# Normalised rows of the first five images on ScalarE, a third input place, and a new order

## The reference

```python
xn = rmsnorm(ln_c(x), g_norm)                  # ln_c: over channels
q, k, v = W_qkv @ xn                           # 4 heads of 32
q = softmax over the head's 32 dims; k = softmax over the 1024 tokens
out = W_out @ (context(k, v) applied to q) + b_out
x = x + rmsnorm(out, g_out)
t = tokens of x
xf = (t - mean) / sqrt(var + 1e-5)             # ln_t: over the 128 channels of a token
probs = softmax(xf @ gate_w + gate_b); the two best of 8 experts per token
t = t + sum over the two of prob * (gelu(xf @ w1[e] + b1[e]) @ w2[e] + b2[e])
```

## Time and profile before

| what | value |
|---|---|
| median of three runs | 755.87 us (751.54 to 756.84) |
| profiled execution | 758.1 us, span 756.4 us |
| PE busy | 658.9 us, 87% |
| DVE busy | 562.6 us, 74% |
| ACT busy | 535.5 us, 71% |
| POOL busy | 481.0 us, 64% |
| mean granted TensorE clock | 0.94 of full |
| HBM traffic | 103.81 MB read, 57.02 MB written |

### The profile page before, as it was taken

How to read it: one execution, slowest core, us unless ns; L and a number is a source line. 1 busy time by engine, 2 the same in 40 slices (tenths; PEclk the granted TensorE clock), 3 DMA queues, 4 the chain that set the end, 5 groups by cost and what they waited for, 6 DMA issues and landing times. The chain is left out here.

```text
span 756.4 us, 15759 instructions
## 1 busy us (share of the span) xinstructions
PE 658.9 (87%) x4074; PEld 545.3 (72%) x4074; DVE 562.6 (74%) x2178; ACT 535.5 (71%) x1388; POOL 481.0 (64%) x504
## 2 busy tenths in 40 slices
PE   3867689889899798999879989998899899998995
PEld 2553478768588577977758867876789788887884
DVE  5889879999899987999778889788679522332342
ACT  2643348787787597879869778686698765676764
POOL 1002635717777677777767777777777775777773
PEclk9987779999999899999989999999699999999997
DMA  7801358458777776896667978884799899659622
GB/s 176 227 19 39 129 183 251 139 175 262 228 201 233 226 230 189 250 271 208 224 218 228 277 224 233 238 262 147 218 282 308 280 294 345 203 149 288 205 78 84
DMA packets 110208, 159.28 MB, mean 211 GB/s; under 512 B 19216, under 2 KB 74536, under 8 KB 110120
## 3 DMA queue, kind: packets, MB, share of 16 engines
q1 hardware_dynamic: 93704, 126.58, 54.7%
q0 software_dynamic: 15360, 31.49, 13.9%
q10 hardware_dynamic: 1056, 0.22, 0.2%
HBM read 103.81 MB, written 57.02 MB: 213 GB/s over the span
## 5 line engine op out<-in xcount | busy, mean ns | idle before, releaser
L840 POOL DMA_INDIRECT rows_in<-xf_tok,row_of x240 | 242.8, 1012 | 179.3 <-DVE row_of L1401 90.9
L855 POOL DMA_INDIRECT y_rows<-rows_out,row_back x240 | 235.8, 982 | 84.6 <-issue 76.5
L1640 PE MATMUL y_ps<-wb,hid 128*128 128x128 f32 x1552 | 207.2, 283 | 17.2 <-ACT hid L957 15.9
L1640 PEld LDWEIGHTS y_ps<-wb,hid 128*128 128x128 f32 x1552 | 189.5, 194 | 36.4 <-ACT hid L957 33.3
L957 ACT ACTIVATE hid<-h_ps,wb 128x256 f32<-128x256 f32 x388 | 162.2, 474 | 55.7 <-PE h_ps L1630 53.1
L1630 PE MATMUL h_ps<-xt,wb 128*128 128x256 f32 x648 | 171.3, 389 | 7.0 <-DMA wb<-experts 5.8
L1630 PEld LDWEIGHTS h_ps<-xt,wb 128*128 128x128 f32 x648 | 114.8, 196 | 21.2 <-DMA wb<-experts 6.9
L1468 DVE TENSOR_TENSOR yb<-y_ps,wb 128x256 f32<-128x256 f32 x162 | 68.0, 420 | 81.2 <-PE y_ps L1640 80.0
L1550 PE MATMUL ab<-wqkv_t,x_sb 128*128 128x392 f32 x256 | 107.8, 556 | 11.9 <-ACT xt L951 4.8
L943 ACT ACTIVATE y_rows<-y_rows,share 128x128 f32<-128x128 f32 x240 | 80.9, 406 | 34.1 <-DMA y_rows<-rows_out,row_back 33.7
L895 ACT ACTIVATE qkv<-ab,root 128x392 f32<-128x392 f32 x128 | 72.4, 589 | 32.7 <-PE ab L1550 26.1
(11 more groups left out here) (195 smaller groups left out, 970.0 us busy)
## 6 DMA issues: line engine op xcount, KB each, us to landing
wb<-experts SPq DMA_DIRECT2D x162, 321.0 KB
xb<-rows_in SPq DMA_DIRECT2D x162, 128.0 KB
rows_out<-yb SPq DMA_DIRECT2D x162, 128.0 KB
rows_in<-zeros SPq DMA_DIRECT2D x69, 128.0 KB, 2.8
x_sb<-in_x_dram SPq DMA_DIRECT2D x16, 512.0 KB, 4.4
out_dram<-out_sb SPq DMA_DIRECT2D x32, 256.0 KB, 3.0
rows_in<-xf_tok,row_of POOLq DMA_INDIRECT x240
y_rows<-rows_out,row_back POOLq DMA_INDIRECT x240
```

The lines of the kernel that those rows point to most:

```text
L840: pool.indirect_dma_start(out=rows_in[p % IN_BUFS], out_offset=bass.IndirectOffsetOnAxis(ap=row_of[:, n % X1_RING, k, t:t + 1], axis=0), i ...
L855: pool.indirect_dma_start(out=y_rows[:, r, k, :], out_offset=None, in_=rows_out[p % OUT_BUFS][0:BLOCKS[p] * ROWS, :], in_offset=bass.Indir ...
L1640: last = pe.matmul(y_ps[:, b % Y_BUFS, i * P:(i + 1) * P], hid[:, b % 2, k, i * P:(i + 1) * P], wb[:, r, HIDDEN + k * CH:HIDDEN + (k + 1) ...
```

## The change

For images 0 to 4 (AIDED = 5) the rows xf are written by ACT as root * x1 + shift, with `shift2` = -mean * root from one new small instruction on DVE. From image 5 on DVE writes them as before; it waits once, at image 5, until ACT has written those of image 4, so that `s_xf` counts in order. POOL's sends wait for the first half of xf before their first tile and for the second before their fifth. `x_sb` has three places in place of two, each with its semaphore. `cw_t` no longer has memory of its own but lies in `square`. All bonuses have new values, so every engine's list may have a new order. The planner gets a few more dependences between steps of neighbouring images.

```diff
-X_RING, TOK_RING, QKV_RING, PAIR_RING = 2, 3, 2, 3
+X_RING, TOK_RING, QKV_RING, PAIR_RING = 3, 3, 2, 3
+AIDED = 5
 ...
-FAVOURED = {...}, FAVOURED_KIND = {...}
+other values for nearly all
 ...
+        if n < AIDED:
+            step("DVE", a("shift2"), 0.1, [a("pair_r")] + old("xf1", 2), 0.12)
         for h in range(2):
-            before = [a("xf0")] if h else [a("pair_r")] + chain("xf1")
+            before = [a("xf0")] if h else [a("shift2" if n < AIDED else "pair_r")] + chain("xf1")
 ...
-            step("DVE", a(f"xf{h}"), 1.02, before, 0.1)
+            step("ACT" if n < AIDED else "DVE", a(f"xf{h}"), 1.5 if n < AIDED else 1.02, before, 0.15, table="any" if n < AIDED else None)
 ...
-            step("POOL", of("send", n, t), 2.49, [a("place"), a("xf1")] + before + ...)
+            step("POOL", of("send", n, t), 2.49, [a("place"), a("xf0" if t < HT else "xf1")] + before + ...)
 ...
-        cw_t = sb("cw_t", [EXPERTS, TOK])
+        cw_t = square[0:EXPERTS, :, :].rearrange("p t c -> p (t c)")
 ...
-        s_x_in = [sem("x_in0"), sem("x_in1")]
+        s_x_in = [sem(f"x_in{r}") for r in range(X_RING)]
 ...
             def send(n, t):
+                if t % HT == 0:
+                    pool.wait_ge(s_xf, n * 2 + 1 + t // HT)
                 if t == 0:
-                    pool.wait_ge(s_xf, n * 2 + 2)
 ...
+                for h in [h for h in range(2) if n < AIDED and what == f"xf{h}"]:      # on ACT
+                    if h == 0:
+                        act.wait_ge(s_shift2, n + 1)
+                        if n >= XF_RING:
+                            m = sent_before(n - XF_RING)
+                            act.wait_ge(s_sent[m % 4], 256 * (m // 4 + 1))
+                    for t in range(h * HT, (h + 1) * HT):
+                        last = act.activation(xf_tok[:, n % XF_RING, t, :], x1_tok[:, n % X1_RING, t, :], ACT.Identity,
+                                              bias=shift2[:, n % 2, t:t + 1], scale=root[:, (n + 1) % PAIR_RING, 1, t:t + 1])
+                    last.then_inc(s_xf, 1)
 ...
+                if what == "shift2":                                                  # on DVE
+                    dve.wait_ge(s_pair, ROOT * (n + 3))
+                    wait(dve, s_xf, (n - 1) * 2)
+                    dve.scalar_tensor_tensor(out=shift2[:, n % 2, :], in0=mean2[:, n % 2, :], scalar=-1.0, in1=r2(n),
+                                             op0=ALU.mult, op1=ALU.mult).then_inc(s_shift2, 1)
-                for h in [h for h in range(2) if what == f"xf{h}"]:
+                for h in [h for h in range(2) if n >= AIDED and what == f"xf{h}"]:
                     if h == 0:
+                        if n == AIDED:
+                            dve.wait_ge(s_xf, n * 2)
```

## The result

| | before | after |
|---|---|---|
| median of 20 runs each, side by side | 755.88 us (749.62 to 759.87) | 751.74 us (747.24 to 757.17) |
| profiled execution | 758.1 us, span 756.4 | 748.99 us, span 747.2 |
| PE, DVE, ACT, POOL busy | 658.9, 562.6, 535.5, 481.0 us | 645.7, 556.2, 546.1, 479.9 us |

The ratio is 0.9952, with an interval of 0.9932 to 0.9973: 4.1 us (0.5%) less, where 8.8 were forecast. The sign was right and the size under half. So the spans differ by 9.2 us where the medians differ by 4.1. I take differences along POOL's queue from the profiles and the total from the medians.

What follows compares the result with a forecast made beforehand. Bound: POOL's indirect-DMA queue, starved by a full DVE until about 172 us. 8.2 (xf off DVE) - 0.4 (shift2) + 1.0 (halves) = 8.8 us less, giving 747.1 against the 755.9 median; range 736 to 762, the forecast's own 742 to 752.

Steps and rivals of the forecast that it cites:

- POOL's queue bounds, and what is won at image 3 carries to the end: POOL's send queue: hardly stops from 171.81 us on, so time won at image 3's addresses carries along it; chance 0.42.
- Since DVE is full, 4 x 2.05 = 8.2 us come off: DVE before image 3's addresses (170.86): removing xf of images 0 to 3 brings them 8.2 us sooner.
- ACT's part at nothing, with 43 us of cover: ACT, 60 to 172 us: 11.2 us of added activations for four images fit its 43 us of idle time, costing nothing.
- The order of everything at 0: All engines: new bonuses reorder everything; taken as 0, between 18.1 us of pause filled and 14 us of new pauses.
- ACT holds DVE and PE: Rival, first four images: rows on ACT delay evictions and Gelus, DVE waits at the means; 16.7 us of stalls, 764.8; chance 0.13.
- The new order fills the third pause: Rival, POOL's 18.1 us pause before image 3: about half filled with image 0's fetches, 738 us; chance 0.18.
- PE holds the end: Rival, after 172 us: stored blocks come no sooner, POOL's 6.9 us pause grows by 8, end stays at 755; chance 0.22.
- The third place: Loading of input x: a third buffer place was taken as worth 0, bounds -2.9 and +1 us.
- the table loads at 0: ACT: no extra table loads expected; rival had two of 1.28 us per image's xf, 752 us, chance 0.05.
- The 1.0 us for the halves: POOL's 1.7 us wait for xf at 306.38: needing only the first half lets it go 1.0 us sooner.
- The signs: Trace checks: xf counts and lengths, image 1's and 3's first sends, DVE's busy share, POOL's later pauses, last fetch near 737.

Runs made afterwards that it cites:

- e9: Kernel before with its order, plus only the third place for x (cw_t in square) and sends waiting by halves; 753.8 us, ratio 0.9996.
- e3: Kernel after, planned with the bonuses of the kernel before; 765.5 us, ratio 1.0160.
- e4: Kernel before, planned with the bonuses of the kernel after; 773.2 us, ratio 1.0254.
- e13: Kernel after with bonuses found by a further search, nothing moved; 744.8 us, ratio 0.9860 to before.
- e5: Kernel before, same order, normalised rows of images 0 to 4 not computed, sends read x1 instead; 757.5 us, ratio 1.0026.
- e2: Kernel after, same order, xf of images 0 to 4 put back on DVE; 762.6 us, ratio 1.0121 to before.
- e15: Order of e13 with the rows of images 0 to 4 back on DVE; 754.9 us, ratio 1.0007 to before.
- e6: Kernel before, same order, xf still on DVE, eight extra unread activations on ACT for each of images 0 to 4; 764.2 us, ratio 1.0115.
- e8: Kernel after, same order, rows of images 0 to 4 not computed, sends read x1 instead; 749.6 us, ratio 0.9946 to before.
- e1: Kernel before, every order kept, xf of images 0 to 4 moved from DVE to ACT at the same planned time; 763.3 us, ratio 1.0113.
- e10: Kernel after, same order, but sends wait for both halves of the rows; 750.6 us, ratio 0.9950 to before.
- e11: Kernel after run once more unchanged, for the spread; 750.9 us, ratio 0.9953 to before.
- e14: Kernel after repeated unchanged in the series of the further searches; 750.9 us, ratio 0.9933 to before.
- e7: Kernel before's order, xf of images 0 to 4 on ACT, images 0 to 3 placed where ACT idled, shift2 behind the root; 759.3 us, ratio 1.0058.
- e12: Kernel before with bonuses found by a further search, nothing moved; 757.9 us, ratio 1.0030.

## Why the sign came true and the working did not

- **POOL's queue bounds, and what is won at image 3 carries to the end: in part.** The two profiles beside each other say so, 573.9 us before, 573.5 after the earlier trace rows. The repeats do not: 574.1 to 576.5 after, and 568.9 for the old order with the small parts (e9). Of some 7 us at image 3, the medians keep 4.1. And it is no law: e3, e4 and e13 have 594.1, 586.3 and 564.5.
- **"Since DVE is full, 4 x 2.05 = 8.2 us come off": wrong, and this is the step that failed.** In the old order the relief is worth 0.3 us at image 3's addresses (e5), since each 2 us became a wait for PE. The 92% in the earlier trace rows was read as a bound. A warning stood in the trace for images 0 and 1: the next wait behind their xf is for PE, and there already was one of 1.3 us each. For images 2 and 3 it took e5 to show it. I looked only at what stood in front of xf, no idle time, which says that nobody keeps DVE waiting there, not that somebody waits for DVE. In the order searched for the move the same work was worth 9.0 us at this gate (e2) and 7.7 in the second such order (e15), which is why image 3 came near the place forecast. That was luck: the working was done on the old order alone.
- **ACT's part at nothing, with 43 us of cover: wrong in the old order (9 us, e6), nearly right in the new one (about 1 us at image 3's addresses, e8).** Idle time in a window covers a step only where the step stands. The price of the step itself was well bounded: 2.8 us an image, 2.7 to 3.3, and 3.18 measured. The estimate of 3.1 us by the Trainium skill, "ScalarE: Activation LUTs", section "What ACT_TABLE_LOAD costs", about 93 ns for each pointer operand, was nearer. The trace agrees roughly: with the second pointer operand the median is 483 ns in place of 402, so 81 ns more.
- **The order of everything at 0: wrong, and for the change as it was made this is the term that is missing.** Without the move the new order costs 7 us (e2), 2.4 of them at image 3's addresses; inside it the move is worth 11. The measured 4.1 is the difference of these two terms, of which the sum had neither. That the forecast came within 5 us is no support for its working.
- **Rivals.** "ACT holds DVE and PE" (0.13), worked out as 764.8, is what e1 and e6 show: 763.3 and 764.2. The number is luck in part: the rival took 16.7 us of stalls less 7.8 of relief, the runs have 9 and 0.3, and DVE waited for PE's results and for ACT's evictions, not for ACT at the means. It did not come because the new order puts ACT's rows elsewhere. "The new order fills the third pause" (0.18) did not happen: image 2's last send starts at 149.00 and POOL then does nothing for 15.25 us. "PE holds the end" (0.22) is not seen: the 6.9 us for stored blocks did not grow but went. What took its place is the 11.7 us before image 6, held by DVE's addresses, which eats what the vanished pauses gave.
- **The small parts.** The third place and the table loads at 0 are borne out (e9; 50 table loads before and after). The 1.0 us for the halves can't be told from 0 (e9: 0.9996, e10 against e11: 0.9950 and 0.9953). shift2 takes 0.17 us, so 0.7 for four images, inside the bounds of 0.3 to 0.8.
- **The signs.** Rows on ACT at 0.35 to 0.5 us, 88 on DVE, image 3's first send near 164 (165.20), the last fetch near 737 (737.74): met, but for another reason than the one given. The pauses behind image 3 sum to 12.8 us, under the 15 named, but to 15.9 in e14. DVE over 90% busy from 60 to 164 failed: 91.6 of 104 us, 88%. Image 1 within 2 us of image 0's end failed: 18.2 us, since the new order brings its addresses at 108.25 for 93.50 and gains the time back at images 2 and 3. The rows alone, placed early enough, bring image 1 forward (95.40 in e7), and no time is won by it; both were forecast.

## What to carry to other kernels

Before a removed instruction is counted as won time, look at the next wait for another engine behind it. If there is one, the removed instruction was filling, and a busy share of 92% does not say otherwise. If there is none, it may still have hidden one (images 2 and 3 here): a run that leaves the instruction out tells. A step that changes its engine in a planned order has one price in the old order (here +8 us) and another in an order searched for it (-10 and -11), so a placement is judged together with its search. And a gain at one gate of a queue counts only together with the pauses behind it: write down the sum of all of them, and from more than one profile.

## What the runs showed of the hardware

One activation of 128 x 128 float32 with a scale and a shift per partition has a mean of 488 ns (median 483), against 406 (median 402) with a scale alone; eight in a row take 3.18 us.

The spread from run to run, 10 us and more for one kernel, goes with the mean granted clock of TensorE. In the 29 runs of before beside e9 to e11 the clock lies between 0.934 and 0.962, and the time falls by 3.8 us for each 0.01 of clock (correlation -0.81); in the 23 beside e12 to e15 it falls by 1.9 us (-0.58). So a difference of 4 us is that of one or two hundredths of clock, and needs its interval. The gain itself is not one of clock: beside e14 the median clock is 0.950 for before and 0.951 for the kernel after, and the ratio is 0.9933. Places within one profile shift too: the kernel after has its first send at 70.16, 66.84 and 70.00 us in three profiles, while from there to image 3's first send it takes 95.04, 94.96 and 93.79 us (before 101.92, and 101.47 in e9). So up to image 3 distances along the queue are a better measure than places. Behind it even distances vary by some 3 us for one kernel (573.5, 574.1 and 576.3 us for the kernel after).
